# Moving the first output piece of a sequence from the fifth pair to the fourth, with a later wait for the last v copy

## What is computed

```python
x = x + attention(layernorm(x))      # 16 heads of 64; softmax(causal(50*tanh(q k / 8 / 50))) v, then Wo
x = x + ffn(layernorm(x))            # shared FFN (gelu) + top 2 of 8 experts, weighed by the gate's softmax
```

## Time and profile before

| | |
|---|---|
| median of 3 runs | 2019.36 us (2017.86 to 2020.98) |
| profiled execution, its own time | 2022.81 us |
| its span, first to last instruction | 2021.0 us, granted PE clock 0.986 |
| DVE, ACT, POOL busy | 75%, 70%, 50% of the span |
| PE waits in the whole span, three largest groups | before L1291 15.4 us, before L1221 10.8 us (once), before L1197 10.8 us |

### The profile page before, as it was taken

One profiled execution on the slowest core, in us unless ns is written; L12 is line 12 of the kernel. 1 busy time (PEld: TensorE's weight loads), 2 busy tenths in 40 slices (PEclk: granted clock), 3 DMA queues, 4 the chain that ended last, 5 costly groups with the idle time before them and its releaser, 6 DMA issues. The chain is left out here.

```text
span 2021.0 us, 40088 instructions
## 1 busy us (share of the span) xinstructions
PE 1915.1 (95%) x14511; PEld 1496.6 (74%) x14511; DVE 1514.7 (75%) x2933; ACT 1414.5 (70%) x2169; POOL 1014.9 (50%) x1195
## 2 busy tenths in 40 slices
PE   6899999999999999999999999999999985998998
PEld 5676767676777777777777777777777754898998
DVE  5577777777878787878777777777777676677777
ACT  6878787878787777777777777777777752444444
POOL 4444555555555545454646464646454542444444
PEclk9999999999999999999999999999999996999999
DMA  4000000000000001010101010101010124665764
GB/s 136 1 12 10 32 22 32 22 33 22 27 27 22 32 17 38 12 43 12 43 12 43 12 43 12 43 12 43 11 43 1 43 74 152 211 189 175 207 196 132
DMA packets 74511, 113.56 MB, mean 56 GB/s; under 512 B 10441, under 2 KB 52942, under 8 KB 74192
## 3 DMA queue, kind: packets, MB, share of 16 engines
q1 hardware_dynamic: 59312, 68.90, 11.5%
q0 software_dynamic: 15008, 42.10, 5.5%
HBM read 64.13 MB, written 48.65 MB: 56 GB/s over the span
## 5 line engine op out<-in xcount | busy, mean ns | idle before, releaser
L523 POOL TENSOR_SCALAR_AFFINE_SELECT prob<-prob 128x256 f32<-128x256 f32 x512 | 222.7, 456 | 651.1 <-ACT prob L613 646.1
L607 ACT ACTIVATE prob<-ring 128x1024 f32<-128x1024 f32 (+1 forms) x384 | 324.1, 874 | 159.7 <-PE ring L1275 152.7
L613 ACT ACTIVATE prob<-prob 128x1024 f32<-128x1024 f32 (+1 forms) x384 | 346.6, 917 | 6.0
L808 DVE TENSOR_TENSOR kT<-ring,kT 64x512 fp32r<-64x512 f32 x256 | 176.3, 689 | 204.2 <-ACT kT L620 171.1
L1291 PE MATMUL bank_o<-prob,v 128*32 128x512 f32 (+3 forms) x4096 | 302.5, 435 | 18.1 <-issue 15.4
L535 POOL TENSOR_TENSOR key_sum<-prob 128x768 f32<-128x768 f32 x128 | 239.4, 1870 | 85.0 <-PE bank_d L1306 68.5
L1291 PEld LDWEIGHTS bank_o<-prob,v 128*32 128x32 f32 x4096 | 116.8, 109 | 184.9 <-issue 174.0
L1270 PE MATMUL ring<-qT,kT 128*128 128x256 f32 (+3 forms) x1024 | 239.9, 336 | 12.4 <-ACT qT L630 8.6
L1270 PEld LDWEIGHTS ring<-qT,kT 128*128 128x128 f32 x1024 | 162.9, 189 | 88.5 <-issue 39.5
L822 DVE RECIPROCAL norm<-bank_d 128x512 f32<-128x512 f32 x64 | 214.7, 3354 | 17.9 <-PE bank_d L1306 17.3
L1275 PE MATMUL ring<-q_lo,kT 128*128 128x256 f32 (+3 forms) x1024 | 227.0, 323 | 0.0
(11 more groups left out here) (222 smaller groups left out, 4654.9 us busy)
## 6 DMA issues: line engine op xcount, KB each, us to landing
xin<-first SPq DMA_DIRECT2D x71, 257.0 KB
xin<-second SPq DMA_DIRECT2D x71, 129.0 KB
xin<-base SPq DMA_DIRECT2D x71, 128.0 KB
x_next<-in_x SPq DMA_DIRECT2D x16, 512.0 KB, 3.9
x_res<-in_x SPq DMA_DIRECT2D x16, 512.0 KB, 3.9
raw_e<-in_w SPq DMA_DIRECT2D x4, 1024.0 KB, 6.6
first<-pad SPq DMA_DIRECT2D x9, 257.0 KB, 6.9
second<-pad SPq DMA_DIRECT2D x9, 129.0 KB, 6.5
```

The lines of the kernel that those rows point to most:

```text
L523: last = nc.gpsimd.affine_select(out=diag, in_=diag, compare_op=ALU.is_ge, fill=0.0, base=0, pattern=[[0, 2], [1, P]], channel_multiplier=-1)
L607: nc.scalar.activation(probs[p % PROBS][u][:, :, :], slot[:, :, 0:UNIT_COLS[u]], ACT.Tanh, scale=SCALE / SOFTCLAMP).then_inc(act_emptied, 1)
L613: nc.scalar.activation(cols, cols, ACT.Exp, scale=SOFTCLAMP).then_inc(exp_done, 1)
L808: last = nc.vector.tensor_tensor(kT[head_rows[1 - h], h, :], slot[r, 1, :], kT[r, h, :].bitcast(F32), ALU.subtract)
```

## The change

Three edits. On PE, `project_out(i, 0)` is done in pair 3, after the projection of q and k and before `values(i, 1)`, for i >= 1 (for i = 0 it stays in pair 4). On DVE, `split_values(i, 0)` comes in pair 3 right after the weighing, ahead of the layer norm's steps and of `empty_qk`; it was behind `empty_qk`. In `values`, the units are sorted by key tile (512, 384, 256, 128 columns; it was 512, 384, 128, 256), in every call, and the first call of a sequence waits at its head for the third v tile only, and for the fourth ahead of its last unit.

```diff
@@ DVE, loop over pairs
                     if p == 2 and i >= 1:
                         split_values(i - 1, PAIRS - 1)
                         add_attention(i - 1)
+                    if p == 3:
+                        split_values(*chunk)
                     if p == 3 and i >= 1:
                         layernorm_guess(2, i - 1)
                         layernorm_newton(2, i - 1)
...
-                    if chunk is not None and p != 1:
+                    if chunk is not None and p not in (1, 3):
                         split_values(*chunk)
@@ PE, values
-                units = [(u, j, at) for u in range(3) for j, at in SCORE_UNITS[u]]
+                units = sorted(((u, j, at) for u in range(3) for j, at in SCORE_UNITS[u]), key=lambda unit: unit[1])
                 if c == 0:
-                    pe.wait_ge(act_emptied, EMPTIED[AT["v", i, NT - 1, 0]][0])
+                    pe.wait_ge(act_emptied, EMPTIED[AT["v", i, NT - 2, 0]][0])
                 pe.wait_ge(masked, 3 * (i * PAIRS + 2 * quad + 1) + 3)
                 for k, (u, j, at) in enumerate(units):
+                    if c == 0 and j == NT - 1:
+                        pe.wait_ge(act_emptied, EMPTIED[AT["v", i, NT - 1, 0]][0])
                     for h in range(QUAD):
@@ PE, loop over pairs
                         project_qk(i + 1, 0)
-                    if p == 4:
+                    if p == (3 if i >= 1 else 4):
                         project_out(i, 0)
```

## The result

The changed kernel runs in 1998.89 us, the median of four runs (1997.19 to 2001.48), where the kernel before has 2018.76 us over four runs beside them. The ratio is 0.9896 (0.9878 to 0.9914): 1.0% faster. In a second set of runs it was 1989.11 against 2007.9 us, a ratio of 0.9903 (0.9886 to 0.9919). I had forecast 14.7 us less; it became 19.9 us by the medians. The ratio times 2019.36 is 1998.4 us, 0.4 us under the low end of my range; the plain median lies 0.1 us inside it. So I missed at the edge of the range, on the side of a larger gain.

A forecast was written before the change was run, and what follows sets the result against it. PE, busy 95% of the span, was taken as the bound: 0.90 + 0.34 - 0.15 - 0.04 - 0.2 = 0.85 us a sequence, times 15, plus 1.9 for sequence 0, gave 14.7 us less, 2004.7 us; range 1998.8 to 2013.4.

The forecast's parts named there:

- wait for the v copy: PE before a sequence's first value call, on ACT's copy of the fourth v tile: all 0.90 us goes, in 15 sequences.
- hole before pair 4's scores: PE's 0.34 us wait for ACT's qT copy closes, as the output piece moves to pair 3.
- ACT's and x2's end before pair 5: ACT's last qT copy (0.15 us) and DVE's x2 low half (0.04 us) take back part of the gain.
- the meeting on DVE: In pair 4 POOL's earlier sum blocks DVE's split of piece 1: 0 to 0.7 us a sequence, taken as 0.2.
- What is late next: ACT's chain through pair 4: its 0.39 us hole closes, pair 5's scores start 1.09 us earlier; after x2, 1.05 remain.
- The split: DVE's cast and subtract, 1.07 us, ahead of pair 3's layer norm, covered by 2.23 us of idle before the kT copy.
- The order of units: All 128 value calls: taken as 0; bounds 14 us lost or gained, from one 0.11 us weight load per call.
- Rival (d): Slower: DVE's moved split waits out POOL's work and four sends on the same data port; 2059 us, chance 0.05.
- The signs: Right: a wait of 0.1 to 0.3 us before pair 5's scores, sequence 0.7 to 1.1 us shorter; wrong: longer value calls.
- Sequence 0: Its first value call's 2.64 us wait for v: some 2.0 us go, taken as 1.9.

The follow-up runs named there:

- e_wait: Kernel before with only the units sorted by key tile and the later wait for the fourth v tile: 2001.62 against 2023.03 us, ratio 0.990.

## Why the prediction was right and wrong

**The mechanism held, the size did not.** Laid over each other by the starts on PE, a sequence gives these terms:

| term | in my sum | measured | from the starts (before; after + 12.41) |
|---|---|---|---|
| wait for the v copy | 0.90 | 1.11 | scores of pair 3: 977.35; 976.24 |
| hole before pair 4's scores | 0.34 | 0.41 | less 1.42 of project_out: 986.05; 985.95 |
| inside pair 4, up to its projection | 0 | 0.20 | 989.25 (row below); 988.95 |
| ACT's and x2's end before pair 5 | -0.19 | -0.45 | plus 1.42 of project_out: 997.69; 996.42 |
| the meeting on DVE | -0.2 | -0.13 | `hidden`: 1008.36; 1007.22 |
| sum | 0.85 | 1.14 | |

The one row of the kernel before that the earlier trace rows lacks, on PE's timeline:

```profile
989.25 0.50 PE L1197 MATMUL ring<-xnTh,w_kh 128*128 128x512 f32 x1 [0.21 <-ACT prob L607]
```

**The wait** was named rightly, "issue" and all: e_wait, the run with it alone, won 1.10 us a sequence. It was nearly the whole forecast as well: my sum left 0.34 - 0.19 - 0.2 = -0.05 us for the moved piece. The step that failed is the size of the wait, together with the start of pair 4 that I worked out from it (below). I took the 0.90 us from the idle column, which counts from the modelled end of the last denominators, 973.33 + 0.83. The kernel after starts the call 0.65 us after the start of that same group, not 0.83. The hole was 975.06 - 973.33 - 0.65 = 1.08 us. That is 0.18 x 15 = 2.7 us of the 5.2 by which the change was worth more than my 14.7. The other 0.03 of the table's 1.11 lie inside the call: up to pair 3's scores it takes 2.27 us now (961.57 to 963.83), 2.29 before.

**The hole before pair 4** closed as forecast. But I set the scores of pair 4 0.18 us later than before; they start 0.10 earlier, again since both holes were larger than their rows. ACT therefore has 0.83 us idle before its first tanh of pair 4 (974.31), where it came straight from the exponentials before, and PE's waits inside the pair shrank by 0.20 us, 3.0 us over 15 sequences. I had this at nothing. With ACT's larger share and the smaller meeting the terms were off by 0.29 us a sequence, 4.4 of the 5.2 us.

**What is late next** was right in kind: ACT's chain, ended by the qT copy that PE now waits for before pair 5. It costs more than my 0.15, for PE got there earlier than I had worked out. It takes back nearly all that the moved piece won: the piece alone is worth 0.06 to 0.08 us, not measurable in the time. That this chain was the limit before pair 5 is shown by taking 1.06 us out of it: the hole went and 0.56 us a sequence came, of which about 0.43 are the hole's and 0.13 those of the meeting that went with it.

**The split** went as worked out: covered, with the cast at 0.80 us beside POOL's last sum, and DVE back at k's low half with no gap. For the rows' normalisation I had 987.18 "at the latest"; it started at 975.09 + 12.41 = 987.50, for it also waits for the POOL sends (of the sequence two back), which I had left out of that bound. DVE idled 2.17 us there. It cost PE nothing: the rows were done at 979.07 and `turn2` took them at 979.46. **The order of units** is worth nothing that its interval (0.9983 to 1.0004) or the length of a call shows. **The meeting**: cast and subtraction took 1.52 and 1.66 us instead of 0.42 and 0.69, ending 0.28 and 0.54 us after POOL's first and second sum. DVE was thus 2.07 us late; I had bounded this by 0.7, from the cast alone, and had left out the subtraction and the second sum. PE paid 0.13 us of it, less than my 0.2, and at another place than I had thought: the low half of `project_out(i, 1)`, right behind pair 5's scores, waits for the subtraction. Its four matmuls take 0.74 us (987.64), where the kernel before has

```profile
1001.31 0.63 PE L1323 MATMUL acc<-w_oh,oTl 128*128 128x256 f32 x4
```

DVE's 2.38 us of idle time covered the rest and were used up: the same L808 now starts without a gap. The rule of the Trainium skill's page "SBUF — State Buffer", section "Who interferes with whom", fits both: the cast waited for a sum that had begun 0.60 us before it, and the subtraction, with two inputs in SBUF, for the next one. Rival (d)'s form of it did not come: the cast ahead of the layer norm ended at 966.80, and did not wait for the sends, the first of which had started at 966.67. The send was not held up by the cast either: it started 0.15 us after POOL's sum, as before, and took 1.00 us (the two overlapped by 0.13 us only).

**The signs.** Two of those that I had named lie just outside their bounds: the wait before pair 5's scores is 0.35 us (0.1 to 0.3), and a sequence is 1.13 us shorter (0.7 to 1.1). None of the signs of being wrong came in the sequences 1 to 15.

**Sequence 0** won what I took, 1.9: from its denominators to the first call of sequence 1 it is 155.87 - 57.29 = 98.6 us before and 151.46 - 55.85 = 95.6 after, and 1.1 of these 3.0 are sequence 1's own wait. In all: 1.14 x 15 + 1.9 = 19.0 us, against 19.9 by the medians and 21 by the ratio. The rest is within what runs of one kernel differ by in the start (0.8 us) and in the expert part (5.6 us), and stays open.

## What to carry to other kernels

When an engine in strict order waits at the head of a group of instructions, look which of them reads the late operand: put that one last and wait there, and the wait costs nothing if the others outlast it. Moving work from a full stage to an empty one only pays if the engine that feeds the next stage has room as well; here it needed an exponential out of that engine's way, and neither edit won anything that the time shows without the other. Price holes from start to start against a place without a hole, not from modelled ends.

## What the runs showed that I had not expected

The idle time before a matmul understates a hole by 0.18 us here: a group of denominators reads 0.83 us, but the next call can start 0.65 us after its start. (The hole of 0.34 us behind a value call was larger than its row by 0.07.) PE's stream loses nothing by a wait in the middle of a value call that is over before PE gets there: the first calls of sequences 1 to 15 take 2.27 us to the next piece with it, and 2.29 with the wait at their head. A call that ends with 128 columns takes as long as one that ends with 256 (2.29 us). One edit to ACT's order paid at two places, since it also took POOL's sums out of the way of DVE's split. And the untouched expert part took 306.4 to 312.0 us in two runs of the same kernel, more than a quarter of what was to be measured.
